# Offset convolution in matmuls of two vertical taps, and w2 summed in the head and made ternary by VectorE

## The reference

```python
# layer 0: deformable 3x3 convolution
om   = conv3x3(y, w_off) + b_off            # y = gn(x); 27 channels: 9 dy/dx offsets, 9 masks
mask = sigmoid(om[:, 18:])
sampled = bilinear(y, grid + offsets) * mask     # 9 taps x 256 channels per pixel
x = x + einsum('bckhw,ock->bohw', sampled, w_conv)
# layer 1: residual block with ternary weights
q1, q2 = ternary(w1), ternary(w2)
out1 = relu(bn(conv3x3(gn(x), q1))); out2 = bn(conv3x3(out1, q2))
x = x + relu(out1 + out2)
# ternary(w): w -= w.mean(); third = (w.max() - w.min()) / 3
#             -1 where w < w.min() + third, 1 where w > w.max() - third, else 0
```

## Time and profile before

| | us |
|---|---|
| median of 3 runs | 2911.25 (2909.43 to 2911.72) |
| the profiled execution | 2900.94 |
| its span in the profile | 2899.2 |
| PE busy in the span | 2443.0 (84%) |
| DVE busy | 2264.2 (78%) |
| ACT busy | 1274.3 (44%) |
| POOL busy | 1440.4 (50%) |
| DMA, mean over the span | 831.07 MB, 287 GB/s |

### The profile page before, as it was taken

One profiled execution on the slowest core, in us unless ns is written; L12 is line 12 of the kernel. 1 busy time (PEld: TensorE's weight loads), 2 busy tenths in 40 slices (PEclk: granted clock), 3 DMA queues, 4 the chain that ended last, 5 costly groups with the idle time before them and its releaser, 6 DMA issues. The chain is left out here.

```text
span 2899.2 us, 38156 instructions
## 1 busy us (share of the span) xinstructions
PE 2443.0 (84%) x12442; PEld 1696.9 (59%) x12442; DVE 2264.2 (78%) x4762; ACT 1274.3 (44%) x2181; POOL 1440.4 (50%) x1270
## 2 busy tenths in 40 slices
PE   4699988869999999899999988998888388999930
PEld 3355555435555666566666655555555388999930
DVE  5788888977888888888888888878886965666665
ACT  3444444445445554555455544444443133322245
POOL 1555555645555565555565556665562803333300
PEclk8799999989999999999999999999898798999965
DMA  8999989988989999999999999998895122111179
GB/s 265 387 348 338 355 334 339 362 295 312 351 336 353 352 354 346 323 346 348 341 354 360 338 349 331 353 342 329 314 337 195 33 86 64 55 52 52 44 288 406
DMA packets 279918, 831.07 MB, mean 287 GB/s; under 512 B 25932, under 2 KB 59724, under 8 KB 279252
## 3 DMA queue, kind: packets, MB, share of 16 engines
q0 software_dynamic: 165888, 604.05, 55.8%
q1 hardware_dynamic: 113876, 225.19, 22.1%
HBM read 743.67 MB, written 85.48 MB: 286 GB/s over the span
## 5 line engine op out<-in xcount | busy, mean ns | idle before, releaser
L503 POOL DMA_INDIRECT G<-pixel_pairs,quad_c x1152 | 1214.7, 1054 | 890.9 <-PE psT L1223 585.8
L995 DVE SCALAR_TENSOR_TENSOR G<-G,wts_c 128x256 f32<-128x256 f32 (+1 forms) x2304 | 1254.7, 612 | 159.2 <-DMA G<-pixel_pairs,quad_c 155.9
L1134 PE MATMUL psD<-ST,wconv 128*128 128x512 f32 x2304 | 1081.3, 614 | 0.0
L602 ACT ACTIVATE G<-G,wts_c 128x256 f32<-128x256 f32 x1152 | 490.2, 497 | 487.9 <-DVE G L995 487.7
L1134 PEld LDWEIGHTS psD<-ST,wconv 128*128 128x128 f32 x2304 | 437.0, 200 | 442.7 <-issue 441.7
L1223 PE MATMUL psT<-idn,G 128*128 128x128 f32 x2304 | 329.9, 290 | 212.1 <-ACT G L602 209.4
L661 ACT ACTIVATE ST<-psT 128x1024 f32<-128x1024 f32 x288 | 293.9, 1020 | 461.1 <-PE psT L1223 460.9
L1223 PEld LDWEIGHTS psT<-idn,G 128*128 128x128 f32 x2304 | 278.7, 149 | 290.8 <-ACT G L602 198.7
L1122 PE MATMUL psF<-pl,qw 128*128 128x256 f32 x1872 | 265.2, 296 | 42.0 <-DVE h1c L852 31.3
L1122 PEld LDWEIGHTS psF<-pl,qw 128*128 128x128 f32 x1872 | 241.3, 192 | 67.0 <-issue 44.8
L1103 PE MATMUL psA<-po,woff 128*64 128x512 f32 x864 | 267.4, 450 | 0.0
(11 more groups left out here) (203 smaller groups left out, 2323.2 us busy)
## 6 DMA issues: line engine op xcount, KB each, us to landing
xx<-in_x SPq DMA_DIRECT2D x56, 512.0 KB, 4.8
pixel_pairs<-yT SPq DMA_DIRECT2D x104, 256.0 KB, 6.1
G<-pixel_pairs,quad_c POOLq DMA_INDIRECT x1152, 6.7
x<-x1c SPq DMA_DIRECT2D x32, 512.0 KB, 5.3
h<-h1c SPq DMA_DIRECT2D x32, 512.0 KB, 10.9
out<-h SPq DMA_DIRECT2D x16, 1024.0 KB, 17.2
xf<-x SPq DMA_DIRECT2D x24, 640.0 KB, 9.3
area<-h SPq DMA_DIRECT2D x24, 640.0 KB, 4.1
```

The costliest lines, as they stand in the source:

```text
L503: pool.indirect_dma_start(out=G[:, i % RING, :], out_offset=None, in_=tbl[d.b].rearrange("y x q c -> (y x) (q c)"), in_offset=bass.Indirec ...
L602: act.activation(g, g, ACT.Copy, scale=wts_c[:, d.p, i:i + 1]).then_inc(d_scaled, 1)
L995: dve.scalar_tensor_tensor(g[:, 0:w], g[:, w:2 * w], wts_c[:, d.p, q * NG + i:q * NG + i + 1], g[:, 0:w], ALU.mult, ALU.add).then_inc(d_ma ...
L1134: ins = pe.matmul(psD[:, oc, :], wconv[:, t, k, oc * 128:(oc + 1) * 128], ST[:, k % 3, t, :], start=(k == 0 and t == 0), stop=(k == TAPS - ...
```

## The change

1. **Offset convolution in 7 units instead of 9 taps** (`off_unit`). `woff` is laid out by dx, then dy, so that the weights of taps dy = 0 and dy = 1 lie side by side: 128 weights columns. A PAIR unit (one per dx) is 4 matmuls of 512 columns whose output rows 0 to 63 hold tap dy = 0 and whose rows 64 to 127 hold tap dy = 1 as seen one image row later. A THIRD unit (one per dx) is 4 matmuls of 512 columns for dy = 2 into rows 0 to 63, with 64 weights columns as before. The CORNER unit is 12 matmuls of 64 columns that give the one image row that the PAIR units lack for dy = 1, in a small accumulator of its own. So 36 matmuls of 512 columns become 24 of 512 and 12 of 64. The tables by k are rewritten: `O_UNITS` and `J_UNITS`.
2. **Evacuation in three copies** (`off_evac`): 64 x 512 with bias, 64 x 448 shifted by one image row, 64 x 64 of the corner. `selhl` has 128 rows and adds all four parts.
3. **New waits of PE**: before a CORNER into `psX`, that ACT has copied the chunk's four transposes (`o_yt`); before one into `psF`, `j_sig`; before `group_sums` in the last chunk with `z`, also `o_omc`.
4. **w2's sums in the head.** SP loads all of w2 (2.36 MB) into the place of `wconv` behind `load_j` and ahead of the table borders; DVE sums it in two halves of 128 x 2304 between its other work of the head; `wconv` is loaded after that (`s_w2p` at 2). The loads and sums of stage 3 are gone; the limits are computed where they were.
5. **Ternary by DVE.** `w2_ternary` on POOL is gone. In the last conv1 stage DVE does `compare_w2` (3 instructions of 128 x 768) between `planes` and `planes_lo` of chunks 2 to 7, and `winograd_w2` (4 instructions of 128 x 768) in chunk 4 behind `planes_lo` and in chunk 7. The loop of that stage is unrolled.

```diff
@@ walk, schedule @@
-            with eng.Fori(0, (NR - 1 - peeled) // 2) as j:
-                emit(2 * j + 1, j, 1, False, False)
-                emit(2 * j + 2, j + 1, 0, False, False)
+            if peeled < NR - 1:
+                with eng.Fori(0, (NR - 1 - peeled) // 2) as j:
+                    emit(2 * j + 1, j, 1, False, False)
+                    emit(2 * j + 2, j + 1, 0, False, False)
...
-            J_TAPS = {5: [0, 1], 6: [2, 3], 7: [4, 5], 8: [6, 7, 8]}
-            O_TAPS = {0: [0], 1: [1, 2], 2: [3, 4], 3: [5, 6], 4: [7, 8]}
+            PAIR, THIRD, CORNER = (0, 4, 5), (1, 2, 3), 6
+            OFF_UNITS = range(CORNER + 1)
+            J_UNITS = {5: [0, 1], 6: [2, 3], 7: [4], 8: [5, 6]}
+            O_UNITS = {0: [0], 1: [1], 2: [2, 3], 3: [4], 4: [5, 6]}
@@ SP @@
                     load_j(Chunk(0, 2, 1, 0, False, False))
+                    sp.dma_start(w2_raw, w2.rearrange("(t c) k o -> c t (k o)", c=128)).then_inc(s_w2l, 16)
                     sp.wait_ge(s_zero, 6)
...
+                    sp.wait_ge(s_w2p, 2)
                     sp.dma_start(wconv[:].rearrange("p t k o -> p t (k o)"),
...
-                    if s == NB - 1 and d.first:
-                        hold(sp, o_tr, PT * NCH + CREDIT)
-                        load_w2(0)
-                    if s == NB - 1 and d.is_row(4):
-                        hold(sp, s_w2p, 3)
-                        load_w2(3)
@@ ACT @@
+                def off_evac(dst, acc, corner):
+
+                    act.activation(dst[0:64, :], acc[0:64, :], ACT.Identity, bias=boff[:, 0:1], scale=1.0)
+                    act.activation(dst[64:128, 0:PX - W], acc[64:128, W:PX], ACT.Copy)
+                    return act.activation(dst[64:128, PX - W:PX], corner[64:128, :], ACT.Copy)
@@ DVE @@
+                def compare_w2(part):
+                    if part == 0:
+                        dve.wait_ge(s_wraw, 16)
+                    raw, q = (m[:, part * 3 * C:(part + 1) * 3 * C] for m in (stage2, above2))
+                    dve.tensor_scalar(q, raw, wall[:, 3:4], wall[:, 6:7], ALU.subtract, ALU.is_gt)
+                    dve.tensor_scalar(raw, raw, wall[:, 3:4], wall[:, 5:6], ALU.subtract, ALU.is_lt).then_inc(s_w2, 1)
+                    dve.wait_ge(s_w2, 2 * part + 1)
+                    dve.tensor_tensor(q, q, raw, ALU.subtract).then_inc(s_w2, 1)
...
+                    dve.tensor_tensor(both, g[0], g[2], ALU.add)
+                    dve.tensor_scalar(g[1], g[1], 0.5, None, ALU.mult).then_inc(s_tern2, 1)
+                    dve.wait_ge(s_tern2, 2 * t + 1)
+                    dve.scalar_tensor_tensor(minus, both, 0.5, g[1], ALU.mult, ALU.subtract)
+                    dve.scalar_tensor_tensor(g[1], both, 0.5, g[1], ALU.mult, ALU.add).then_inc(s_tern2, 1)
...
                             planes(f2)
+                            if not f.first:
+                                compare_w2(f.r - 1)
                             planes_lo(s, f2)
+                            if f.is_row(4):
+                                winograd_w2(0)
+                        if s == NB and f.last and k == 2:
+                            winograd_w2(1)
@@ PE @@
+                def off_unit(pad, acc, corner, unit):
+
+                    dx = unit - 3 if unit in (4, 5) else unit - 1 if unit in THIRD else 0
+                    for t in range(CT):
+                        for part in range(2):
+                            begin, end = t == 0 and part == 0, t == CT - 1 and part == 1
+                            if unit in PAIR:
+                                ins = pe.matmul(acc.rearrange("p (h w) -> p h w", h=RC), woff[:, t, dx, 0:2, :].rearrange("p y m -> p (y m)"),
+                                                pad[:, part, t, 0:RC, dx:dx + W], start=(dx == 0 and begin), stop=(dx == 2 and end))
+                            elif unit in THIRD:
+                                ins = pe.matmul(acc[0:64, :].rearrange("p (h w) -> p h w", h=RC), woff[:, t, dx, 2, :],
+                                                pad[:, part, t, 2:2 + RC, dx:dx + W], start=False, stop=False)
+                            else:
+                                for x in range(3):
+                                    ins = pe.matmul(corner, woff[:, t, x, 0:2, :].rearrange("p y m -> p (y m)"),
+                                                    pad[:, part, t, RC, x:x + W], start=(x == 0 and begin), stop=(x == 2 and end))
```

131 lines of the change are left out of this document (53 added, 78 removed).

## The result

The changed kernel takes 2832.95 us (median of 4 runs, 2830.75 to 2835.05) where the kernel before takes 2910.34 in the same comparison: a ratio of 0.9735, with a 95% interval of 0.9718 to 0.9752. That is 77 us less, where the prediction had 52. The profiled execution of the changed kernel took 2835.05 us, its span 2833.3, so it lies 2 us above its median.

What follows compares the result with a forecast made beforehand. No engine is full; each stage is bound by the wait that ends last, such as the deformable ring or PE waiting for DVE. Terms -42 - 13 + 6 - 10 + 7 = -52 gave a median of 2859 us, range 2836 to 2880.

Steps and rivals of the forecast that it cites:

- A: Last conv1 stage: ternary by DVE instead of POOL removes PE's waits for DVE, -42 us, bounds -47 and -31.
- The stalls: Last conv1 stage: two PE waits left, 1.9 us ahead of chunk 2 and 3.3 us in chunk 4.
- rival 2: Last conv1 stage: compares lengthen DVE's chunk by their full 2.4 us, saving only 31 us; time 2870, chance 0.11.
- B: Stage 3: without w2's sums and second load, chunks 4 and 5 become like chunk 3, -13 us, bounds -10 and -14.
- C: Head: w2's 2.36 MB load ahead of the table writes delays the first gather, +6 us, bounds +3 and +9.
- The lower bound: Head, +3 us: the DMA share leaves 0.07 free, and DMA stands still some us ahead of w2's load.
- D: Stage 0: offset convolution saves 2.9 us a chunk, counted as 2 in five chunks, -10 us, bounds -14 and -3.
- my row: Profile row of 27-column matmuls with 128 weights columns, 0.125 us each, used to price CORNER at 1.5 us.
- E: Stages 1 and 2: offset convolution's savings waited away, losses behind tap 4 and ACT's copies count, +7 us, bounds -3 and +10.
- the rule: Stages 1 and 2: PE work saved ahead of tap 4 is waited away; PE work behind it counts in full.
- Rival 1: Everywhere: PE is the bound, so PE work saved is time saved, -43 us for the offset convolution; time 2819, chance 0.08.
- Rivals 3 and 4: CORNER's matmuls: 3, nearly free, time 2834, chance 0.07; 4, slow at 0.38 us each, time 2932, chance 0.03.

Runs made afterwards that it cites:

- e2: Kernel before with only w2's ternary values made by DVE in the last conv1 stage: 2864.47 us, ratio 0.9851.
- e10: Changed kernel with GpSimd also running eight instructions of the old ternary's kinds and sizes on the unneeded wconv: 2881.21 us, ratio 0.9901 of before.
- e3: Kernel before with only w2 loaded and summed in the head: 2899.77 us, ratio 0.9975.
- e5: The changed kernel run again as it is, against the kernel before: 2830.39 us, ratio 0.9742.
- e9: Changed kernel with w2's load ahead of the waiting third-chunk load and the first winograd_w2 in the last chunk: 2824.05 us, ratio 0.9717 of before.
- e1: Kernel before with only the offset convolution changed to units: 2881.23 us, ratio 0.9913.
- e4: Changed kernel with stream o's units issued earlier, none behind tap 4: 2845.80 us, ratio 0.9793 of before.
- e13: Kernel before without two of stream o's nine convolution taps, one behind tap 1 and one behind tap 3: 2891.17 us, ratio 0.9942.
- e14: Kernel before without one of stream o's two convolution taps behind tap 4: 2901.64 us, ratio 0.9978.
- e15: Kernel before with only PE's transposes of y issued ahead of the same tap's convolution taps: 2899.15 us, ratio 0.9976.

## Why the prediction was off

**A, the ternary on DVE: right.** -42 was predicted, e2 alone gives -42 by the medians. The stalls came smaller than predicted (0.55 and 2.15 for 1.9 and 3.3) by 2.5 us. The compares fit in the gap, which refutes rival 2. The mechanism, GpSimd's activity slowing DVE, is shown by e10. What I had not read is how: by whole instructions, a DVE instruction lasting about as long as the one it met. The Trainium skill has this rule, in SBUF — State Buffer, section Who interferes with whom: DVE and GpSimd share one pair of ports, which the one that starts first holds for its whole instruction. The trace of e10 agrees for the long rows (16.07 us for a compare of 0.67) and not for the compare at 2250.10, which takes its 0.67 us though GpSimd's row has begun 0.26 earlier.

**B, the sums out of stage 3: right.** -13 predicted, -13.7 in e3 and in the changed kernel.

**C, w2 in the head: right within its bounds, and with a miss of its own.** +6 predicted; at the end of chunk 0 +7 to +8 in e3, +4.5 in the changed kernel, +3 to +4 in e5. But the first gather, where the whole price was to show, is only 3.2 to 3.6 us late in these three; what e3 loses behind it was not looked into. The lower bound already named the DMA engines' standing time ahead of the load, and took it for room that the load could use where it stood. It couldn't, as it was issued behind the wait that causes it. e9 moved it and the cost was gone.

**D, stage 0: right sign, too small.** Predicted -10; -13.7 in the changed kernel, -15.3 to -16.3 in e1. Two terms were mis-sized. First the price: with CORNER at 1.25 instead of 1.5 and 0.2 saved at each of the two turnings of the offsets, which I had not counted, the matmuls of chunk 1 stand 3.6 us a chunk closer together, not 2.9. For the 1.25 us the section LDWEIGHTS of the Trainium skill's page TensorE: Matmul & The Clock Gate was nearer than my row: its rule, weights columns over 1.2 in ns, is 107 ns for 128 columns, an estimate of 1.28 for the twelve, and the trace agrees with it. Second the share that reaches the time: in e1, against e2, chunks 1 to 5 are 2.6 us shorter in the mean where I had counted 2, and chunks 6 and 7, which I had at nothing, 2.8 together.

**E, stages 1 and 2: no loss where one was forecast.** Predicted +7; e1 gives -4.3 to -5.1 against e2 and e3. By the scatter of single profiles the sign is not certain (against before's own profile it is +1.9), but +7 is out: with the 16 us of stage 0 and the 4.5 of stage 3 it would make e1 13 to 14 us faster, and its medians have 25 (21 to 30 by the interval). This is the step that failed: "up to tap 4 the chain DVE to ACT sets the pace, and PE work saved before it turns into PE waiting; behind tap 4 [...] its work counts in full". e4 moves work from behind tap 4 to ahead of it and is 15 us slower where the rule says 20 to 30 faster. e13 takes 1.96 us a chunk away ahead of tap 4 and gains 8 to 9 us in these stages where the rule says 0; e14 takes 0.98 away behind it and gains 3 to 4 where it says 14, and 6 in all where it says 19. The 0.13 us between ACT's end and PE's start showed that ACT came last, but not why. ACT's own chain had waited for PE's transposes of y, as the waits show (150.8 us in e4, 134.3 in e2, 88.2 in e1, 41.8 in e15) and e15: moving these transposes alone, with no work taken away, brings 8 us by the medians. Behind tap 4 the price was too high as well: by the rows of chunk 1 of stage 0, +0.32 for the units and -0.20 for the turning are +0.12, where I had +0.52 and 1 us for ACT.

**The base.** I added the 10 us between the profiled run of before and its median to both kernels alike. 6 to 7 of them lay in stages 1 and 2: 1069.6 us in that run, 1075.8 and 1076.6 in e2 and e3. That is why the profiles of before and after show +1.3 us for E. Rival 1 (PE's work counts everywhere) is wrong too, on the other side: it had 43 us for what e1 measured as 25. Rivals 3 and 4 fall with CORNER's price, 0.104 us a matmul, between theirs and near to the 0.125 that I took. Rival 3's time, 2834, is within 2 us of the measured one all the same: it had D at -20 and E at -8, more than e1 shows, for a reason that isn't there, and that the sum fits is luck.

The measured 2832.95 lies 3 us below the range's lower end. Of the 25 us that were missing, e1 carries 22: by its profile 5 to 6 in D, 11 to 12 in E, and 4.5 in stage 3, for a reason that stays open.

## What to carry to other kernels

That engine X released engine Y last, by a hair, says nothing of whether work taken from Y is lost. Follow X's own chain back, over every in-order instruction ahead of it; where one of them waits for Y, X's time is Y's time too. Where two such paths are of nearly one length, work taken away counts by a part (here a quarter to six tenths) and work added by more (here three quarters), so a saving should be priced at a part and not at nothing, and the best place of a piece of work is to be found by trying both neighbours.

A helper engine that can hold another one up, as GpSimd did here with DVE, is judged by the length of its single instruction and not by its busy share. Cutting its instructions freed the other engine (46 us of loss became 16), but then look at what stands behind them in its own queue.

## What the runs showed of the hardware that was not expected

A DVE instruction of 0.67 us on SBUF, one tensor in and one out, can last 16.07 us beside a GpSimd instruction of 16.51 us on another tile; a DVE instruction with an operand in PSUM took its usual 0.41 beside one of 4.31. In pieces of 256 columns GpSimd's compares took twice their time (1.86 against 0.91 us for as many elements; 1.21 at the shortest, 3.35 at the longest, beside `planes_lo`), and DVE lost up to some 0.4 us an instruction beside them.

Four float32 matmuls of 27 columns, eight in the profile, took 1.00 us with 64 weights rows and 0.80 us with 128. Twelve float32r ones of 64 columns with 128 weights rows and columns took 1.25 us, 0.104 each against 0.100 for 27 columns, so the moving columns made next to no difference.
